# One-hot tiles made by two fp16 tensor comparisons a block, and the first feature steps issued earlier

## What is computed

```python
...
x = -0.0002949 + 1 * normal(1250, 512);  N = 1250 nodes, E = 41250 edges sorted by dst
edge_index = jnp.stack([src, dst])
xn = _layernorm(x, axis=-1)
x = x + gnn(xn, edge_index, node_vec1, ...) + mix(xn[None], ...)[0]
x = x + ffn(_layernorm(x, axis=-1)[None], ...)[0]

# mix: the first part of the program, where the change lies
def softmax_kernel(x, pmat):
    xp = jnp.einsum('bhnd,df->bhnf', x, pmat)              # 8 heads of 64, 256 features
    xp = xp - jnp.max(xp, axis=-1, keepdims=True)
    return jnp.exp(xp) / math.sqrt(pmat.shape[-1])
h = layernorm(x, g1, be1)
qkv = h @ Wqkv + bqkv
q_prime = softmax_kernel(q, Pmat)
k_prime = softmax_kernel(k, Pmat)
kv = jnp.einsum('bhnf,bhne->bhfe', k_prime, v)
k_sum = jnp.sum(k_prime, axis=2) + 1e-06
z = 1.0 / jnp.einsum('bhnf,bhf->bhn', q_prime, k_sum)[..., None]
attn = jnp.einsum('bhnf,bhfe->bhne', q_prime, kv) * z
x = x + attn @ Wproj + bproj
mlp = jax.nn.gelu(layernorm(x, g2, be2) @ W1 + b1, approximate=False) @ W2 + b2

# gnn: 4 layers of attention over the edges
scores = jnp.einsum('ehd,ehd->eh', q[src], k[dst])
smax = jax.ops.segment_max(scores, src, num_segments=N)
ex = jnp.exp(scores - smax[src])
denom = jax.ops.segment_sum(ex, src, num_segments=N)
out = jax.ops.segment_sum((ex / denom[src])[:, :, None] * v[dst], src, num_segments=N)
```

## Time and profile before

| | us |
|---|---|
| median of 3 runs | 2411.66 (2403.01 to 2413.3) |
| the profiled execution's own time | 2415.14 |
| span of its profile | 2413.2 |
| PE busy | 2363.5 (98%) |
| DVE busy | 1412.7 (59%) |
| ACT busy | 962.9 (40%) |
| POOL busy | 923.0 (38%) |

### The profile page before, as it was taken

One profiled execution on the slowest core, in us unless ns is written; L12 is line 12 of the kernel. 1 busy time (PEld: TensorE's weight loads), 2 busy tenths in 40 slices (PEclk: granted clock), 3 DMA queues, 4 the chain that ended last, 5 costly groups with the idle time before them and its releaser, 6 DMA issues. The chain is left out here.

```text
span 2413.2 us, 27609 instructions
## 1 busy us (share of the span) xinstructions
PE 2363.5 (98%) x9345; PEld 1401.6 (58%) x9345; DVE 1412.7 (59%) x2944; ACT 962.9 (40%) x1663; POOL 923.0 (38%) x1271
## 2 busy tenths in 40 slices
PE   8999999999999999999999999999999999999998
PEld 4565655546677556577556577666567664543443
DVE  7897671432776653677554487555377555633435
ACT  5886643221665221466221276321166422212221
POOL 2005203030565330365341075452056543436674
PEclk9999999999999999999999999999999999999999
DMA  5401101230566310366310166510056601769417
GB/s 168 139 19 32 45 14 52 86 112 18 125 156 164 128 59 18 78 155 161 89 43 22 44 160 159 137 43 22 18 140 159 181 35 55 260 199 350 146 42 229
DMA packets 132171, 257.23 MB, mean 107 GB/s; under 512 B 49503, under 2 KB 51279, under 8 KB 129692
## 3 DMA queue, kind: packets, MB, share of 16 engines
q1 hardware_dynamic: 85102, 150.39, 21.3%
q0 software_dynamic: 45584, 102.75, 15.3%
q10 hardware_dynamic: 1346, 2.33, 0.3%
HBM read 212.95 MB, written 31.98 MB: 101 GB/s over the span
## 5 line engine op out<-in xcount | busy, mean ns | idle before, releaser
L114 POOL DMA_DIRECT2D cols<-w x720 | 354.0, 499 | 573.9 <-PE psum L655 338.6
L684 PE MATMUL psum<-cols,rows 128*128 128x256 f32 (+1 forms) x1600 | 369.2, 379 | 0.0
L670 PE MATMUL psum<-g_k_cols,g_q_cols 128*125 128x512 f32 (+1 forms) x960 | 360.6, 513 | 0.0
L684 PEld LDWEIGHTS psum<-cols,rows 128*128 128x128 f32 (+1 forms) x1600 | 303.3, 190 | 39.9 <-issue 4.2
L875 ACT ACTIVATE g_prob<-g_prob,g_row_max 125x1250 f32<-125x1250 f32 x160 | 214.0, 1337 | 239.2 <-DVE g_row_max L788 236.9
L788 DVE CUSTOM_DVE_ANT_0 g_prob<-psum,ln_count 125x1250 f32<-125x1250 f32 x160 | 233.5, 1459 | 105.4 <-PE psum L670 105.4
L670 PEld LDWEIGHTS psum<-g_k_cols,g_q_cols 128*125 128x125 f32 x960 | 179.4, 187 | 171.3 <-issue 163.0
L802 DVE STREAM_TRANSPOSE w<-g_prob 128x1280 f32<-128x1280 f32 x160 | 241.5, 1510 | 42.2 <-DMA cols<-w 24.0
L881 ACT ACTIVATE g_prob<-g_prob,g_row_max 125x1250 f32<-125x1250 f32 x160 | 214.1, 1338 | 107.3 <-DVE g_row_max L778 107.3
L2831 PE MATMUL psum<-m_ew,m_x_cols 128*64 128x256 f32 (+1 forms) x576 | 152.1, 495 | 1.4 <-DMA cols<-in_L_ffn_expert_w,m_weights_of 0.8
L741 PE MATMUL psum<-w,g_k_cols 128*125 128x512 f32 x320 | 143.6, 592 | 0.0
(11 more groups left out here) (395 smaller groups left out, 3948.9 us busy)
## 6 DMA issues: line engine op xcount, KB each, us to landing
cols<-w POOLq DMA_DIRECT2D x720, 80.0 KB, 3.2
cols<-w SPq DMA_DIRECT2D x560, 80.0 KB
w<-in_L_gnn_m_w SPq DMA_DIRECT2D x8, 1024.0 KB
slot_rows<-p_kf SPq DMA_DIRECT2D x1, 7128.0 KB, 32.6
rows<-slot_rows SPq DMA_DIRECT2D x54, 132.0 KB
m_ew<-in_L_ffn_expert_w SPq DMA_DIRECT2D x4, 1536.0 KB, 11.8
slot_outputs<-slot_rows SPq DMA_DIRECT2D x1, 5000.0 KB
w<-in_L_mix_W SPq DMA_DIRECT2D x4, 1024.0 KB, 5.2
```

Source lines behind the costliest of these rows:

```text
L114: return eng.dma_start(out, in_, allow_slow_non_contiguous=True)
L670: ins = pe.matmul(psum[0:P, at:at + width], q_cols[:, h, t * P:(t + 1) * P], k_cols[:, h, start:start + width], start=True, stop=True)
L684: ins = pe.matmul(c.bank(6 + g % 2, 256).rearrange("p (u a i) -> p u a i", u=2, a=SIDE), rows[0:r, j, h * 128:(h + 1) * 128], turned_keys[ ...
```

## The change

The one-hots of a block's first 6 tiles are made by two DVE instructions, `tensor_tensor` with `is_equal`: one over 6 tiles x 128 source columns, one over 6 x 256 key columns. Their operands are `iota`, read again for each tile, and a new table `repeated`, which holds every key 8 times in fp16 so that both operands have an innermost run of 8. ACT fills this table, two copies for each set of 10 blocks (`repeat_keys_act`). ACT has 2 tiles in every block (100 of 400), and one-hots are 128 and 256 wide. `sum_pe` waits for the whole of DVE's block ahead of its first matmul. `key_features(0..2)` stand in PE's queue ahead of `sum_pe(49)`; `query_features(0)` and `(1)` stand among the last key steps; the turned kv tiles go through banks 4 and 5 by turns, two ahead of the second query step's exponentials and two behind. A one-column exponential stands at the head of ACT's attention. `h_norm_dve(0)` stands ahead of the last division. The remaining edits (renamed semaphores, banks 6 and 7 in `count_tile`, DVE's `highest(0)` and `highest(1)` behind the last key maxima) follow from these.

```diff
+    HOT_DVE, SAME = W - 2, 8
+    SRC_COLS, KEY_COLS = 128, 256
+    SET_BLOCKS = BLOCKS // SETS
...
+        HOT = SRC_COLS + KEY_COLS
+        hots = shared[0:P, 0:W * HOT].bitcast(F16).rearrange("p (u k n) -> p u k n", u=2, n=HOT)
+        repeated = shared[0:P, W * HOT:W * HOT + 2 * SET_BLOCKS * HOT_DVE * SAME].bitcast(F16).rearrange(
+            "p (u n b f) -> p u n b f", u=2, n=2, b=SET_BLOCKS)
...
-        def dve_tiles(b):
-
-            return W - 2 if b % 3 == 2 else W - 1
-
-        def hots_before(b):
-            return sum(dve_tiles(i) for i in range(b))
+        def repeat_keys_act(s_):
+
+            s = c.act
+            if s_ == 0:
+                s.wait_ge(keys_copied, 2)
+            if s_ >= 2:
+                s.wait_ge(hot_made, 2 * SET_BLOCKS * (s_ - 1))
+            of = slice(s_ * SET_ROWS, (s_ + 1) * SET_ROWS)
+            for n in range(2):
+                s.copy(repeated[:, s_ % 2, n].rearrange("p b (k c) -> p b k c", c=SAME),
+                       edge_cols[:, n, of].rearrange("p (b k) -> p b k", k=W)[:, :, 0:HOT_DVE].unsqueeze(3).broadcast_to(
+                           [P, SET_BLOCKS, HOT_DVE, SAME])).then_inc(keys_repeated, 1)
         def hot_dve(b):
             v = c.dve
+            s_, at = divmod(b, SET_BLOCKS)
+            if at == 0:
+                v.wait_ge(keys_repeated, 2 * (s_ + 1))
             if b >= 2:
                 v.wait_ge(summed, b - 1)
-            for k in range(dve_tiles(b)):
-                hot = hots[:, b % 2, k, :]
-                e = b * W + k
-                v.tensor_scalar(hot[:, 0:P], iota[:, 0:P], edge_cols[:, 0, e:e + 1], None, ALU.is_equal).then_inc(
-                    hot_made, 1)
-                v.tensor_scalar(hot[:, P:], iota[:, :], edge_cols[:, 1, e:e + 1], None, ALU.is_equal).then_inc(hot_made, 1)
+            for n, (c0, width) in enumerate(((0, SRC_COLS), (SRC_COLS, KEY_COLS))):
+                shape = [P, HOT_DVE, width // SAME, SAME]
+                v.tensor_tensor(hots[:, b % 2, 0:HOT_DVE, c0:c0 + width].rearrange("p k (j c) -> p k j c", c=SAME),
+                                iota[:, 0:width].rearrange("p (j c) -> p j c", c=SAME).unsqueeze(1).broadcast_to(shape),
+                                repeated[:, s_ % 2, n, at].rearrange("p (k c) -> p k c", c=SAME).unsqueeze(2).broadcast_to(shape),
+                                ALU.is_equal).then_inc(hot_made, 1)
         def hot_act(b):
             s = c.act
             if b >= 2:
                 s.wait_ge(summed, b - 1)
-            made = W * b - hots_before(b)
-            for k in range(dve_tiles(b), W):
-                hot = hots[:, b % 2, k, :]
-                for n, part in enumerate((hot[:, 0:P], hot[:, P:])):
-                    s.activation(part, iota[:, 0:(P, KEYS)[n]], ACT.Abs,
-                                 bias=away_cols[:, n, b, k - W + 2:k - W + 3]).then_inc(hot_apart, 1)
-            for k in range(dve_tiles(b), W):
-                hot = hots[:, b % 2, k, :]
-                made += 1
+            for k in range(W - HOT_DVE):
+                hot = hots[:, b % 2, HOT_DVE + k, :]
+                for n, part in enumerate((hot[:, 0:SRC_COLS], hot[:, SRC_COLS:])):
+                    s.activation(part, iota[:, 0:(SRC_COLS, KEY_COLS)[n]], ACT.Abs,
+                                 bias=away_cols[:, n, b, k:k + 1]).then_inc(hot_apart, 1)
+            for k in range(W - HOT_DVE):
+                hot = hots[:, b % 2, HOT_DVE + k, :]
+                made = (W - HOT_DVE) * b + k + 1
                 s.wait_ge(hot_apart, 2 * made)
                 s.activation(hot, hot, ACT.Relu, bias=1.0, scale=-1.0).then_inc(hot_act_made, 1)
@@ -1693,13 +1709,13 @@
                 pe.wait_ge(keys_copied, 2)
             else:
                 pe.wait_ge(counted, b - 1)
+            pe.wait_ge(hot_made, 2 * (b + 1))
             for k in range(W):
-                if k < dve_tiles(b):
-                    pe.wait_ge(hot_made, 2 * (hots_before(b) + k + 1))
-                else:
-                    pe.wait_ge(hot_act_made, W * b - hots_before(b) + k - dve_tiles(b) + 1)
+                if k >= HOT_DVE:
+                    pe.wait_ge(hot_act_made, (W - HOT_DVE) * b + k - HOT_DVE + 1)
                 hot = hots[:, b % 2, k, :]
-                ins = pe.matmul(c.bank(6 + b % 2, KEYS, P), hot[:, 0:P], hot[:, P:], start=(k == 0), stop=(k == W - 1))
+                ins = pe.matmul(c.bank(6 + b % 2, KEYS), hot[:, 0:SRC_COLS], hot[:, SRC_COLS:SRC_COLS + KEYS],
+                                start=(k == 0), stop=(k == W - 1))
...
+                    if b == BLOCKS - 1:
+                        for n in range(3):
+                            key_features(n)
                     sum_pe(b)
...
                         hot_act(b + 2)
+                    if b % SET_BLOCKS == 2 and b // SET_BLOCKS + 1 in range(2, SETS):
+                        repeat_keys_act(b // SET_BLOCKS + 1)
...
+        def key_features(n):
+
+            pe = c.pe
+            if n == 0:
+                pe.wait_ge(p_in, 32)
+                pe.wait_ge(k_made, GROUPS)
+                pe.wait_ge(q_made, GROUPS - 2)
+            elif n == 1:
+                pe.wait_ge(q_made, GROUPS)
+            elif n == 2:
+                pe.wait_ge(cond_made, 3)
+            else:
+                pe.wait_ge(kf_made, 4 * (n - 2))
+            g, u = divmod(n, NT // 2)
+            for b in range(2):
+                for e in range(2):
+                    ins = feature_pe(kf_out(n)[:, e, b, :], k_cols, e, g, 2 * u + b)
+            ins.then_inc(kf_mm, 1)
+
+        def query_features(n):
+            pe = c.pe
+            if n < 2:
+                pe.wait_ge(kf_made, 4 * (K_STEPS - 1 + n))
+            else:
+                pe.wait_ge(qf_made, 4 * (n - 1))
+            g, u = divmod(n, NT // 2)
+            for b in range(2):
+                for e in range(2):
+                    ins = feature_pe(qf_out(n)[:, e, b, :], q_cols, e, g, 2 * u + b)
+            ins.then_inc(qf_mm, 1)
+
         def attention_pe():
             pe = c.pe
-            pe.wait_ge(q_made, GROUPS)
-            pe.wait_ge(k_made, GROUPS)
             pe.wait_ge(counted, BLOCKS)
-            pe.wait_ge(cond_made, 3)
-            pe.wait_ge(p_in, 32)
             pe.wait_ge(ones_made, 1)
-            for n in range(K_STEPS + S_LAG):
-                if n < K_STEPS:
-                    g, u = divmod(n, NT // 2)
-                    if n >= 3:
-                        pe.wait_ge(kf_made, 4 * (n - 2))
-                    for b in range(2):
-                        for e in range(2):
-                            ins = feature_pe(kf_out(n)[:, e, b, :], k_cols, e, g, 2 * u + b)
-                    ins.then_inc(kf_mm, 1)
+            for n in range(2, K_STEPS + S_LAG):
+                if 3 <= n < K_STEPS:
+                    key_features(n)
+                elif K_STEPS <= n < K_STEPS + 2:
+                    query_features(n - K_STEPS)
...
+                if g >= 2:
+                    pe.wait_ge(kv_cols_made, g - 1)
                 for n in range(4):
-                    ins = pe.transpose(c.bank(g)[:, n * 128:(n + 1) * 128], kv_t[:, g, n * 128:(n + 1) * 128], ident[:])
+                    ins = pe.transpose(c.bank(4 + g % 2)[:, n * 128:(n + 1) * 128], kv_t[:, g, n * 128:(n + 1) * 128], ident[:])
                 ins.then_inc(kv_turned, 1)
...
-                if n >= 1:
-                    pe.wait_ge(qf_cols_made, 2 * n)
+                pe.wait_ge(*((qf_cols_made, 2 * n) if n else (kv_cols_made, G)))
...
-            for n in range(Q_STEPS):
-                features(n)
-                if n >= 1:
-                    turn_features(n - 1)
+            for n in range(1, Q_STEPS):
+                if n >= 2:
+                    query_features(n)
+                turn_features(n - 1)
                 if n >= 2:
                     attend(n - 2)
...
+            v.wait_ge(qf_turned, 2 * Q_STEPS)
+            h_norm_dve(0)
             divide(Q_STEPS - 1)
...
             s = c.act
+            s.wait_ge(ones_made, 1)
+            s.activation(warm[:], ones[:, 0:1], ACT.Exp)
...
+            def query_exp(n):
+                s.wait_ge(qf_max, n + 1)
+                if n >= 2:
+                    s.wait_ge(qf_turned, 2 * (n - 1))
+                else:
+                    s.wait_ge(kv_mm, K_STEPS - 1 + n)
+                    s.wait_ge(kf_summed, K_STEPS - 1 + n)
+                for i in range(4):
+                    s.activation(kf[:, 4 * (n % 2) + i, :], qf_out(n)[:, i // 2, i % 2, :], ACT.Exp,
+                                 bias=mx[:, 4 * (n % 2) + i:4 * (n % 2) + i + 1]).then_inc(qf_made, 1)
+
+            for n in range(2):
+                query_exp(n)
+                for g in (2 * n, 2 * n + 1):
+                    s.wait_ge(kv_turned, g + 1)
+                    s.copy(kv_flat[:, g, :], c.bank(4 + g % 2)).then_inc(kv_cols_made, 1)
+            for n in range(1, Q_STEPS + 1):
+                if n >= 3:
```

(8 more changed lines are left out.)

90 lines of the change are left out of this document (32 added, 58 removed).

## The result

The changed kernel takes 2415.61 us (median of 12 runs, 2412.04 to 2421.56), the kernel before, beside it on the same chip, 2405.19 (12 runs, 2401.80 to 2413.30). The ratio is 1.0044, 95% interval 1.0033 to 1.0055: slower by 8 to 13 us, within the 0.5% that the forecast called no change. The profiled execution took 2416.76 us with a span of 2415.0. Before's profiled execution (2415.14) was some 10 us above before's own median; the two spans differ by only 1.8 us and can't be compared as wholes, because the stages that the change doesn't touch differ from trace to trace: from the fourth query features to the end they take 2156.2 us in before's trace, 2145.8 in after's, and 2142.3 to 2152.1 in those of the experiments. What can be compared is the stretch from the first Q/K/V group to the steady query steps.

The account below looks back on a forecast made before the run. In the projection DVE was slowest by a little, PE next, ACT with room. +12.7 + 1.7 - 2.6 - 4.0 = +7.8 us on the profiled 2415.14 gives 2422.9, less 3.5 for the runs' median: 2419.5 (own range 2412 to 2426).

Parts of the forecast that it names:

- ACT's part: Projection: 34 more tiles and the key copies make ACT the engine that sets the end; last count 12.7 us later.
- DVE's rate: Projection: the two new comparisons take 1.7 us a block, a middle between 0.9 and 2.65; ACT hides it either way.
- The fp32 row: Projection: the trace's fp32 tensor_tensor, 1.15 ns an element, as the slow end for the new comparisons: 2.65 us a block.
- The start: Last count to first kv step: 3.3 us in place of 5.9, so 2.6 us come back.
- The features ahead of `sum_pe(49)`: End of projection: two key feature steps stand ahead of the last block's sums and delay the last count by 1.7 us.
- The key steps: First kv step to last key exponentials: no difference forecast, 0 us.
- The second rival: Projection: waits for ACT bring half-clock stretches, costing PE about 1.7 us each, say 2 to 5 us: 2424; chance 0.10.
- The drain: Last key exponentials to fourth query features: the new order starts the fourth step's features at 253.0 against 257.00, 4.0 us gained.
- Rival 4: Projection: ACT's added 37.8 us fit beside PE and DVE, PE's 14.0 us of waits go: 2391; chance 0.06.
- the first rival: Projection: DVE at the fp32 rate or below, 0.8 us in each of six three-block groups, +5: 2424, or 2434; chance 0.16.

Follow-up runs that it names:

- ACT's load alone: The kernel before, with ACT making two tiles in every block (100 of 400) by the old comparisons: 2412.65 us, ratio 1.0027.
- even blocks: The kernel before, with two blocks behind each of the 24 groups in place of one, two or three: 2408.79 us, ratio 0.9994.
- the run that fills this hole: The changed kernel, with unread matmuls, six ahead of the first kv step and four behind the turned kv tiles: 2414.02 us, ratio 1.0022 to the kernel before.
- seven tiles: The changed kernel, with seven tiles a block on DVE (runs of 4) and one on ACT: 2401.09 us, ratio 0.9984 to the kernel before.

## Why the prediction held, and which of its steps did not

The time forecast, 2419.5, is 3.9 us off, inside its range, and on the right side. But two of the table's five rows failed, 1.6 and 3.4 us too low, and they were covered by luck, by the median that the forecast was set against: 2411.66 of three runs, where twelve gave 2405.19. As a change, +7.8 was forecast, +10.4 measured (8 to 13), +13.1 in the trace.

**ACT's part: right, in size and in kind.** "ACT becomes the engine that sets the end, and the last count ends 12.7 us later", with the features 14.4: from the first group the last count ends 14.6 us later. Two tiles were put at 2.19 us and took 2.21; the copies of the keys were put at 0.55 us each:

```profile
L1672 ACT CAST p_shared<-p_edge_sum 125x480 f16<-125x480 f32 x6 | 3.2, 585 | 0.0
```

585 ns each with the tail. ACT's waits for PE went from 22.1 to 3.5 us, 2.8 of them for the last count, and adding ACT's load alone did 9.6 of the 13.0. That PE would wait for Relu (L1704) and not for the comparisons (L1685) is what the lists show: 14.2 us of the weight loads' waits against none, and 6.7 us of the matmuls' against 2.3. One reading was off: a copy counted 0.52 us that needs 0.42 has a tail of 0.10, not "some 0.13", so the room was some 26 us and not 27; the sum would have been 1 us higher.

**DVE's rate: the estimate was high, and it mattered more than said.** The middle taken was 1.7 us a block; measured 1.39. The fp32 row would have given 2.65. The Trainium skill (VectorE: DVE Perf Modes, "The perf-mode tier table (the rule you actually need)") has such a comparison at twice the fp32 rate; the estimate by it was 1.4 (half of 2.65 is 1.33), and this trace agrees. "The sum does not rest on it" fits what was measured at 1.39 us; at 2.7 it costs 5 us, and 1.7 was not run.

**The start: right, and one term in part by luck.** Last count to first kv step 3.40 us, forecast 3.3, by the very parts: 0.3 branch, 1.28 load, 0.11 to the exponentials, 1.70 to kv. The features ahead of `sum_pe(49)`: the row of the table is 1.6 longer, forecast 1.7. But the two steps hold PE for 1.93 us (199.40 to 201.33) behind a wait of 0.56, and before's own row of 4.58 held three waits for DVE of 0.33 us each. With ACT's load alone the row is 3.24 us; with before's one-hots and the features it is 5.43.

**The key steps: a term that the sum lacked.** The forecast left them at 45.15 us. Moving the features ahead of the last block left PE with nothing between its last one-hot matmul and the first kv step, 3.8 us (the wait in the row at 206.16). The clock then fell to 0.50 from about 206 us, over kv steps and features that set the pace. Before, it fell at 190, over features behind which PE waited anyway for the table load and the exponentials, and the key steps were 45.15 us long, as they are with even blocks, where it didn't fall there at all. The price is 1.6 us, shown by the run that fills this hole. But before's order does not keep it away: with ACT's load alone the clock fell at 201.7, over the key steps, and cost the same 1.6. The second rival had the mechanism, but looked for it in the projection. There it does occur, one window in which PE works at 0.50:

```profile
186.00:188.00 2.00, 2.00 (x7) 1.60 (x6) 1.43 (x2) 2.00 (x7) 0.00 (x0) 0.50 0.00 0
```

and another from 83.2 us. They lie beside ACT's work, as the rival said. Since ACT stands idle for only 0.7 us in the whole stretch, they can have made it at most that much longer.

**The drain: "Gain 4.0 us" failed; it was 0.6.** 1.6 us is the clock: the turn at 265.38 takes 1.93 us where 1.04 is usual. The rest, 1.8, is order, and would be 2.6 if before's drain had not had its own stretch at half clock (16.89 with it, 16.13 without). The forecast turned the kv tiles at 244.1, 4.0 us behind the start of the last key exponentials; they are turned 258.41 - 252.89 = 5.5 us behind it. Query features 1 and the last kv and key sums stand ahead of them on PE, and the delay of the latter was put down as covered by ACT's copies. But the copies come behind the turned tiles: all that follows, copies at 259.10 and first turn at 262.76, moved with them. The first turn comes 9.9 us behind the start of the last key exponentials, where the forecast had 8.5; the other 0.5 lies between it and the fourth features, 4.9 us at full clock (260.98 to 265.86 in the run with added matmuls) where the forecast had 4.4.

**Rival 4 could not have given 2391.** Its price was PE's 14.0 us of waiting weight loads. With all of these gone, PE gained 9.1 us. A load may wait while the matmul ahead of it still runs; by these two numbers a third of the waits did. Nor was taking ACT's load off enough to get it: seven tiles gave 2.4 of the 9.1, until the blocks were spread evenly. In the forecast's words "PE now waits for a whole block of DVE, not for a tile" stood with the first rival alone, at 0.8 us a group; with seven tiles, and DVE at its fast rate, it costs 6.3 us in the six groups, 1.05 us each on average. The same arithmetic says how the change could have gained: it moved 34 tiles to ACT, which had 104 us of work in the stretch, in order to relieve DVE, whose new commands had brought it from 112.6 us to 67.

What stays open: how exactly the 3.4 us between the run with ACT's load alone and the changed kernel divide between the copies and the rest; why the clock fell in the drain of some traces and not of others with the same order; and why the stages behind differ by up to 14 us from trace to trace.

## What to carry to other kernels

When an engine gets a faster command, work out anew which engine has room and deal the work by that; here the same comparisons made the kernel 0.44% slower with six tiles a block on DVE, and 0.54% faster with seven and an even order. A coarser hand-over (a block for a tile) needs its consumer's demand to be even: look for the place where three pieces are asked for in the time of two. When work is moved forward out of a wait, look at what the engine then does in the hole that is left: a stretch at half clock that used to fall on work with slack may fall on the path. Before a gain of a microsecond or two is put down to an order, look in both traces at where the clock was 0.50.

## What was not expected of the hardware

- The busy time of TensorE held 7.5 us of stalls: 119.3 us for 571 matmuls that need 111.8 without a wait, beside only 1.5 us of idle time. Between one-hot matmuls the starts are 107 ns apart; before, 29 were 360 ns apart, DVE's pace.
- A weight load of 125 columns took 136 ns, one of 128 columns 98, with 125 rows in fp16 in both; it made 0.3 us of difference.
- Six small fp32 matmuls in the hole of 3.8 us ahead of the first kv step kept the granted clock at 1.00 afterwards, and cost nothing that the trace shows.
- DVE's comparisons were slow or stood still while GpSimd worked. In before's trace a comparison of 125 columns, usually 0.25 us, took 2.44 us beside GpSimd's tensor_tensor; beside its memsets the comparisons took 0.55 and 0.70 us in place of 0.26 and 0.29, and from 186 us PE waited for them, before the clock fell at 190. In the changed kernel, too, a comparison of 768 elements, usually 0.55 us, took 2.74 us beside the same tensor_tensor. No run takes GpSimd's work away. From before's timeline:

```profile
78.27 2.44 DVE L1669 TENSOR_SCALAR p_shared<-iota,p_edge_sum 125x125 f16<-125x125 f16 x1
78.27 2.38 POOL L1288 TENSOR_TENSOR ln_count<-ln_count 16x1250 f32<-16x1250 f32 x1 [23.54 <-ACT ln_count L1463]
...
184.87 2.60 POOL L1150 MEMSET cols<- 18x512 f32 x4 [104.22 <-PE psum L1730]
...
186.39 0.55 DVE L1669 TENSOR_SCALAR p_shared<-iota,p_edge_sum 125x125 f16<-125x125 f16 x1
186.85 0.70 DVE L1671 TENSOR_SCALAR p_shared<-iota,p_edge_sum 125x250 f16<-125x250 f16 x1
186.95 0.32 PE L1702 MATMUL psum<-p_shared 125*125 125x250 f16 x1 [0.32 <-DVE p_shared L1669]
```
